# One low half of the transposed norm made on TensorE and copied by ScalarE, and the tile map of a routed mixture cut into four parts

## What is computed

```
x = x + ssm(layernorm(x))        # Bu = x B^T; h_t = a*h_{t-1} + Bu_t; y = h C^T + D*x
n = layernorm(x)
logits = n @ gate_w.T            # 8 experts
top_id, score = argmax(logits), sigmoid(max(logits))
x = x + swiglu_shared(n) + swiglu_{top_id}(n * score)   # hidden width 256
```

## Time and profile before

| | us |
|---|---|
| median of 3 runs | 280.53 (279.43 to 281.22) |
| the profiled execution | 280.06 |
| its span, first to last instruction | 277.8 |
| around the span | 2.26 |
| busy: PE / PEld | 235.3 (85%) / 181.2 (65%) |
| busy: DVE / ACT / POOL | 177.2 (64%) / 172.3 (62%) / 146.1 (53%) |

### The profile page before, as it was taken

How to read it: one execution, slowest core, us unless ns; L and a number is a source line. 1 busy time by engine, 2 the same in 40 slices (tenths; PEclk the granted TensorE clock), 3 DMA queues, 4 the chain that set the end, 5 groups by cost and what they waited for, 6 DMA issues and landing times. The chain is left out here.

```text
span 277.8 us, 6120 instructions
## 1 busy us (share of the span) xinstructions
PE 235.3 (85%) x1891; PEld 181.2 (65%) x1891; DVE 177.2 (64%) x512; ACT 172.3 (62%) x415; POOL 146.1 (53%) x150
## 2 busy tenths in 40 slices
PE   0595979979779999999599899999999999999900
PEld 0254466566457456767276799999999999765700
DVE  3799998799887976659952256655555565534200
ACT  2844898887897965633134889776777684523400
POOL 1000000027777757778781036777777777775950
PEclk9999597979999999999889999999999999999975
DMA  7999500002323222323944924454555443211992
GB/s 207 383 355 327 211 0 2 1 19 100 116 99 115 105 78 99 119 97 119 318 150 139 296 94 120 136 165 128 176 170 168 132 119 107 77 49 48 106 172 26
DMA packets 24862, 37.83 MB, mean 136 GB/s; under 512 B 3680, under 2 KB 16864, under 8 KB 24272
## 3 DMA queue, kind: packets, MB, share of 16 engines
q1 hardware_dynamic: 15264, 22.03, 25.9%
q0 software_dynamic: 9568, 15.41, 19.9%
HBM read 22.03 MB, written 19.73 MB: 150 GB/s over the span
## 5 line engine op out<-in xcount | busy, mean ns | idle before, releaser
L1045 POOL DMA_INDIRECT table<-rows,place x64 | 65.8, 1027 | 61.9 <-DVE place L815 43.0
L1086 POOL DMA_INDIRECT out<-w_full x51 | 49.3, 967 | 32.9 <-DVE w_full L1015 18.6
L441 PE MATMUL bank<-xT_hi,w_split 128*128 128x256 f16 (+1 forms) x156 | 41.1, 264 | 0.5 <-DVE xT_lo L1000 0.5
L443 PE MATMUL bank<-xT_hi,w_split 128*128 128x256 f16 (+1 forms) x156 | 41.1, 264 | 0.0
L442 PE MATMUL bank<-xT_lo,w_split 128*128 128x256 f16 (+1 forms) x156 | 40.9, 263 | 0.0
L593 ACT ACTIVATE n1T<-bank,g_scale 128x512 f32<-128x512 f32 x32 | 21.8, 687 | 28.8 <-PE bank L395 22.7
L453 PE MATMUL bank<-w_full,hid 128*128 x284 | 38.6, 277 | 0.2
L453 PEld LDWEIGHTS bank<-w_full,hid 128*128 128x128 f32 x284 | 34.8, 192 | 1.5 <-issue 0.4
L871 DVE SCALAR_TENSOR_TENSOR hid<-bank,h_scale,n1T 128x512 f32<-128x512 f32 x32 | 23.3, 747 | 15.3 <-ACT n1T L593 14.3
L407 PEld LDWEIGHTS bank<-w_full,hid 128*128 128x128 f32 x256 | 31.4, 195 | 2.1 <-issue 0.3
L407 PE MATMUL bank<-w_full,hid 128*128 128x128 f32 x256 | 31.5, 277 | 0.0
(11 more groups left out here) (142 smaller groups left out, 439.5 us busy)
## 6 DMA issues: line engine op xcount, KB each, us to landing
w_full<-table SPq DMA_DIRECT2D x24, 264.0 KB, 4.0
rows<-in_x SPq DMA_DIRECT2D x8, 512.0 KB, 7.6
w_full<-in_weights SPq DMA_DIRECT2D x3, 1152.0 KB, 12.0
table<-in_pads SPq DMA_DIRECT2D x1, 2112.0 KB, 9.2
table<-in_pads SPq DMA_DIRECT2D x8, 264.0 KB, 4.5
x_ring<-table SPq DMA_DIRECT2D x8, 264.0 KB, 3.8
out<-rows POOLq DMA_DIRECT2D x8, 256.0 KB, 7.9
table<-rows,place POOLq DMA_INDIRECT x64, 2.4
```

Source lines behind the costliest of these rows:

```text
L441: mm(o, w_of(kind, e, 0, c), xT_hi[k][:, 0:w], start=True, stop=False)
L443: last = mm(o, w_of(kind, e, 1, c), xT_hi[k][:, 0:w], start=False, stop=True)
L1045: g.indirect_dma_start(table[:, :], bass.IndirectOffsetOnAxis(ap=place[:, i:i + 1], axis=0), rows[:, i, :], None).then_inc(done, 16)
L1086: g.indirect_dma_start(out[:, :], bass.IndirectOffsetOnAxis(ap=x_in[k][:, s, 2 * D:2 * D + 1].bitcast(I32), axis=0), x_in[k][:, s, 0:D], N ...
```

## The change

1. `minus_one`, the identity times -1 in 16 bits, is made once by ACT in step -1, ahead of `norm1(0)`. `std1(1)` moves in ACT's step -1 from between `norm1(0)` and `copy_n1T(0,0)` to behind `copy_n1T(0,1)`.
2. Block 1 of every pair is no longer transposed by PE's transpose but by a matmul with the identity that opens an accumulation in bank 6. For pairs 0 to 6 PE then adds `minus_one` times `n2T_hi` to the bank (`rest_n2`), so the bank holds the low half, and ACT copies it to `n2T_lo` (`rest_lo`). DVE's `split_lo` makes the low half of block 0 alone, except in the last pair. `rest_n2(s-1)` stands on PE behind `skip(s+1)`; `rest_lo(s-1)` stands on ACT between `std2(s)` and `norm2(s,0)`. In step 7 `rest_n2(6)` comes behind `shared_gate_up(0)`.
3. `ranks(2)` moves on PE from ahead of `shared_down(1)` to behind `shared_down(0)`, and `places(2)` on DVE from behind the hidden values of block 2 to behind `base(0)`.
4. `tile_map` is cut in four, at b = 7, 9, 10 and 11, behind the hidden values of these blocks. The instructions are the same.

The core of the diff (the bodies of the map's parts are as they were):

```diff
             def transpose_n2(q, b):
                 pe.wait_ge(s_n2, q * 2 + b + 1)
-                after(pe, s_lo, q * 2 + b - 1)
+                after(pe, s_lo[b], q)
                 for t in range(BT):
                     i = q * PT + BT * b + t
-                    last = nc.tensor.transpose(bank[5 + b][:, P * t:P * (t + 1)], n2[:, i, :], identity)
+                    o = bank[5 + b][:, P * t:P * (t + 1)]
+                    if b == 0:
+                        last = nc.tensor.transpose(o, n2[:, i, :], identity)
+                    else:
+                        last = mm(o, n2[:, i, :], identity, start=(t == 0), stop=(t == BT - 1))
                 last.then_inc(s_t2, 1)
+            def rest_n2(q):
+                if q == 0:
+                    pe.wait_ge(s_minus, 1)
+                pe.wait_ge(s_hi, q * 2 + 2)
+                mm(bank[6][:], minus_one[:], n2T_hi[:, (q * 2 + 1) * SEQ:(q * 2 + 2) * SEQ],
+                   start=False, stop=True, skip_group_check=True).then_inc(s_rest, 1)
...
                     skip(s + 1)
+                if 1 <= s < LAST:
+                    rest_n2(s - 1)
...
             for b in range(FIRST):
                 shared_gate_up(b)
+                if b == 0:
+                    rest_n2(LAST - 1)
...
-                if b == 2:
-                    ranks(GROUPS - 2)
...
                     shared_down(b - 1)
+                if b == 1:
+                    ranks(GROUPS - 2)
...
+            def rest_lo(q):
+                act.wait_ge(s_rest, q + 1)
+                run(n2T_lo[:, (q * 2 + 1) * SEQ:(q * 2 + 2) * SEQ], bank[6][:], ACT.Copy).then_inc(s_lo[1], 1)
...
+                if s == -1:
+                    act.wait_ge(s_const, 16)
+                    run(minus_one[:], identity, ACT.Copy, scale=-1.0).then_inc(s_minus, 1)
                 if -1 <= s < LAST:
                     norm1(s + 1)
-                if s + 2 < PAIRS:
+                if s + 2 < PAIRS and s != -1:
                     std1(s + 2)
...
                     copy_n1T(s + 1, 1)
+                if s == -1:
+                    std1(1)
...
                     std2(s)
+                if s >= 1:
+                    rest_lo(s - 1)
                 if 0 <= s < LAST:
                     norm2(s, 0)
                     norm2(s, 1)
...
             def split_lo(q):
-                for b in range(2):
+                for b in range(2 if q == LAST else 1):
...
-                if b == 2:
-                    places(GROUPS - 2)
                 if 1 <= b <= EARLY:
                     base(b - 1)
+                if b == 1:
+                    places(GROUPS - 2)
...
                 if b == 7:
-                    tile_map()
+                    map_counts()
+                if b == 9:
+                    map_singles()
+                if b == 10:
+                    map_experts()
+                if b == 11:
+                    map_rows()
```

More of the change, by code:

```diff
@@ L114, in block_kernel @@
         d_diag = sb("d_diag", [P, P])
+        minus_one = sb("minus_one", [P, P], F16)
         w_max = sb("w_max", [P, 3])
@@ L223, in block_kernel @@
         s_r2, s_nb2, s_n2 = sem("r2_steps"), sem("nb2_ready"), sem("n2_ready")
-        s_t2, s_hi, s_lo = sem("n2_transposed"), sem("n2T_hi_ready"), sem("n2T_lo_ready")
+        s_t2, s_hi = sem("n2_transposed"), sem("n2T_hi_ready")
+        s_lo = [sem("n2T_lo_first_ready"), sem("n2T_lo_second_ready")]
+        s_minus, s_rest = sem("minus_one_ready"), sem("n2T_rest_ready")
         s_logit, s_route = sem("logits_ready"), sem("route_steps")
@@ L349, in logits @@
                     pe.wait_ge(s_parked, 2)
-                pe.wait_ge(s_lo, (g + 1) * GROUP * 2)
+                pe.wait_ge(s_lo[0], (g + 1) * GROUP)
+                pe.wait_ge(s_lo[1], (g + 1) * GROUP)
                 after(pe, s_before, g)
@@ L384, in shared_gate_up @@
                 tok = slice(block_of(b) * SEQ, (block_of(b) + 1) * SEQ)
-                pe.wait_ge(s_lo, block_of(b) + 1)
+                pe.wait_ge(s_lo[block_of(b) % 2], block_of(b) // 2 + 1)
                 for c in range(FC):
@@ L778, in split_lo @@
                     v.tensor_tensor(out=n2T_lo[:, tok], in0=bank[5 + b][:], in1=n2T_hi[:, tok],
-                                    op=ALU.subtract).then_inc(s_lo, 1)
+                                    op=ALU.subtract).then_inc(s_lo[b], 1)
             def route(g):
@@ L919, in _, with map_ready, map_spread, map_counts @@
                     route(s // GROUP - 1)
[L920 to L932, removed]
+            map_steps = [0]
+            def map_ready(instruction):
+                instruction.then_inc(s_map, 1)
+                map_steps[0] += 1
+                dve.wait_ge(s_map, map_steps[0])
+            def map_spread(values, n):
+                return values[:, None, :].to_broadcast([P, n, E])
+            def map_counts():
                 dve.wait_ge(s_count, 1)
-                ready(v.tensor_copy(pad_place[:], count_bank))
-                ready(v.tensor_tensor(out=count_f[:], in0=count_bank, in1=region_of, op=ALU.subtract))
+                map_ready(v.tensor_copy(pad_place[:], count_bank))
+                map_ready(v.tensor_tensor(out=count_f[:], in0=count_bank, in1=region_of, op=ALU.subtract))
                 v.memset(end_whole[:, 0:1], 0.0)
@@ L939, in tile_map @@
                 v.tensor_scalar(halves_i[:], count_f[:], float(P - 1), None, ALU.add)
-                ready(v.tensor_tensor(out=whole_i[:], in0=count_f[:], in1=round_up, op=ALU.add))
+                map_ready(v.tensor_tensor(out=whole_i[:], in0=count_f[:], in1=round_up, op=ALU.add))
                 v.tensor_scalar(halves_i[:], halves_i[:], P.bit_length() - 1, None, ALU.arith_shift_right)
-                ready(v.tensor_scalar(whole_i[:], whole_i[:], SLOTS.bit_length() - 1, None, ALU.arith_shift_right))
+                map_ready(v.tensor_scalar(whole_i[:], whole_i[:], SLOTS.bit_length() - 1, None, ALU.arith_shift_right))
@@ L943, in tile_map @@
                 v.tensor_copy(halves_f[:], halves_i[:])
[L944 to L949, removed]
@@ L950, in tile_map, with map_singles @@
-                ready(v.tensor_scalar(single[:], single[:], 0.0, None, ALU.max))
+                map_ready(v.tensor_copy(whole_f[:], whole_i[:]))
+                map_ready(v.tensor_tensor_scan(end_whole[:, 1:E + 1], ones_e, whole_f[:], 0.0, ALU.mult, ALU.add))
+            def map_singles():
+                map_ready(v.tensor_scalar(end_whole[:, 1:E + 1], end_whole[:, 1:E + 1], float(WHOLE), None, ALU.min))
+                map_ready(v.tensor_tensor(out=whole[:, 0:E], in0=end_whole[:, 1:E + 1], in1=end_whole[:, 0:E],
+                                          op=ALU.subtract))
+                map_ready(v.scalar_tensor_tensor(out=single[:], in0=whole[:, 0:E], scalar=-2.0, in1=halves_f[:],
+                                                 op0=ALU.mult, op1=ALU.add))
+                map_ready(v.tensor_scalar(single[:], single[:], 0.0, None, ALU.max))
@@ L951, in tile_map @@
                 v.tensor_scalar(first_single[:], whole[:, 0:1], 2.0, None, ALU.mult)
                 v.tensor_scalar(whole_gain[:], whole[:, 0:E], -2.0, float(PITCH), ALU.mult, ALU.add)
[L953 to L956, removed]
+                map_ready(v.tensor_tensor_scan(end_single[:], ones_e, single[:], 0.0, ALU.mult, ALU.add))
@@ new lines, in map_singles, with map_experts @@
+                map_ready(v.scalar_tensor_tensor(out=next_gain[:], in0=whole[:, 1:E + 1], scalar=2.0, in1=whole_gain[:],
+                                                 op0=ALU.mult, op1=ALU.add))
+                map_ready(v.tensor_tensor(out=single_gain[:], in0=next_gain[:], in1=single[:], op=ALU.subtract))
+            by_whole = (slice(0, WHOLE), end_whole[:, 1:E + 1], whole_gain[:])
+            by_single = (slice(WHOLE, TILES), end_single[:], single_gain[:])
+            def map_experts():
@@ L959, in tile_map @@
                     number = const[:, col["tile_no"]][:, 0:n]
-                    ready(v.tensor_tensor(out=ended[:, tiles, :], in0=spread(end, n),
-                                          in1=number[:, :, None].to_broadcast([P, n, E]), op=ALU.is_le))
-                ready(v.tensor_reduce(tile_expert_f[:], ended[:], AX, ALU.add))
+                    map_ready(v.tensor_tensor(out=ended[:, tiles, :], in0=map_spread(end, n),
+                                              in1=number[:, :, None].to_broadcast([P, n, E]), op=ALU.is_le))
@@ L963, in tile_map @@
+                map_ready(v.tensor_reduce(tile_expert_f[:], ended[:], AX, ALU.add))
                 for tiles, end, gain in (by_whole, by_single):
                     n = tiles.stop - tiles.start
-                    ready(v.tensor_tensor(out=ended[:, tiles, :], in0=ended[:, tiles, :], in1=spread(gain, n), op=ALU.mult))
+                    map_ready(v.tensor_tensor(out=ended[:, tiles, :], in0=ended[:, tiles, :], in1=map_spread(gain, n),
+                                              op=ALU.mult))
```

(13 more changed lines are left out.)

## The result

The changed kernel takes 290.31 us (median of 6 runs, 288.51 to 291.07), the kernel before 280.21 (6 runs, 279.19 to 281.38): 1.034 times as long, 95% interval 1.032 to 1.037. Where executions of a kernel fell into a longer group at a lower granted clock, ratios leave them out. The profiled execution took 290.9, its span is 288.7, so 10.9 more span than before.

A forecast was written before the change was run, and what follows sets the result against it. Pair stage bound by a loop through ACT, routed stage by PE and POOL, first tile by POOL's chain. 280.06 + 10.4 (POOL's chain) + 1.5 + 0.6 (clock) = 292.6, taken as 292.5 us; range 285 to 300.

The forecast's parts named there:

- The new wait: On ACT ahead of norm2(s), rest_lo waits for rest_n2 behind skip(s+1): second copy to norm2 4.5 us instead of 2.1.
- The length of the loop: ACT's pair-stage loop becomes 11.85 us; after five loops norm2(6) starts at 98.75 instead of 85.92, +12.8.
- What ACT waits for: Pair stage before: ACT idles once a step, 0.88 to 1.21 us for nb from DVE, with no other gap.
- std1's move: Kernel start: std1(1) behind the copy makes DVE's scan start 1.1 us later, carried on to norm2(0).
- POOL: Block 8's scatter at 113.7, POOL's chain +10.4 us, its two long scatters stay, tile at 164.8.
- a wait of several us: Sign on POOL: the scatter of block 8 would stand behind a wait of several us for place.
- The clock in the steps: Pair stage: more waiting of PE in every step lowers its clock; half of a full loss taken, 1.5 us.
- Rival C: Low clock in every pair-stage step: six losses of 1.5 us, 9 in place of 1.5, time 300; chance 0.14.
- The clock ahead of the tiles: PE waits about 3 us ahead of the first tile and its clock falls: 0.6 us lost.
- The map: Tile map in parts: stall of 3.44 and slow pitch go, 5.7 us off PE's chain, but this buys nothing.
- places: On DVE, place of group 2 comes 1.8 us sooner, ahead of two hidden values, for POOL's scatter of block 8.
- Rival A: Pair stage: DVE sets the pace, 0.6 us comes back each step, POOL's wait of 2.07 goes: 276.2; chance 0.06.

The follow-up runs named there:

- Run 1: Changed kernel with PE's rest product ahead of skip instead of behind it: 278.19 us, 0.996 of the kernel before.
- run 3: Changed kernel with std1(1) back in its old place, ahead of the first copy of n1T: 288.30 us, 1.034 of the kernel before.
- run 9: Kernel before with only the tile map cut in four parts, third chip: 279.88 us, 1.0034 of the kernel before.
- run 10: Kernel before with only places and ranks of the third group moved, third chip: 278.50 us, 0.9954 of the kernel before.
- runs 4: Kernel before with places and ranks moved and the tile map in four parts, no identity product: 279.39 us, 0.9995 of the kernel before.
- run 8: Changed kernel with rest product ahead of skip and std1(1) in its old place, on the slow chip: 332.08 us, 1.013 of the kernel before.
- run 12: Changed kernel with rest product ahead of skip and std1(1) in its old place, on the third chip: 278.02 us, 0.9959 of the kernel before.

## Why the prediction was right

290.3 was measured, 292.5 forecast, inside the range of 285 to 300, with the mechanism named. The profiled execution was 10.9 longer than before, where the sum had 12.5. Step by step:

- **The new wait** was as worked out, with its place. Forecast 4.5 us from the second copy to norm2; measured at full clock 99.82 + 0.50 - 95.88 = 4.4. Run 1 shows the cause: taking skip out of the wait alone brings the time back.
- **The length of the loop.** norm2(6) was forecast at 98.75 plus 1.5 of clock, 100.25; it came at 100.32. So close a match is in part luck: norm2(1) came 0.4 sooner than forecast (38.34), the three loops at full clock were 11.7, 12.0 and 11.6 long (forecast 11.85, though its own terms add up to 11.80), and the clock took 0.7 more than its term.
- **What ACT waits for.** "Everything else in ACT's step has no gap" holds for step 5, which was read, and not for all: in step 4 of the kernel before ACT also waited 0.74 us for PE's transposes (62.52).
- **std1's move**: forecast 1.1, measured 1.10 at norm2(0) in run 3.
- **POOL**: forecast 113.7 plus 1.5, 115.2, for the scatter of block 8; measured 115.65, behind `place`. The sign "a wait of several us" did not come: it was 2.78 us, before 2.37. POOL was free of its first 32 scatters at 112.86 and not at 107 to 109, since `keep_step` held it back for 2.32 and 2.14 us in them. Had `place` come much sooner still, no more than 2.5 us would have been gained. The 32 scatters from there took 42.8 us instead of 43.9, because their two long ones were shorter (4.0 together, before 5.4). This was the mis-sized term: I had kept both as they were. The tile followed the last scatter by 6.85 instead of 7.13 us, and so came at 165.30, not at 166.3.
- **The clock in the steps**: 1.5 forecast, 2.2 paid in this execution, by gaps 1.0 and 1.2 us longer. The granted clock, third number from the end, shows that the half level came in three stretches of the pair stage:

```profile
45.00:55.00 10.00, 8.88 (x93) 5.68 (x93) 5.16 (x23) 6.34 (x17) 0.00 (x0) 0.83 0.01 2
55.00:66.00 11.00, 8.30 (x41) 4.72 (x39) 8.96 (x32) 7.08 (x19) 0.00 (x0) 0.84 0.00 1
76.00:86.00 10.00, 8.78 (x90) 6.31 (x89) 6.05 (x28) 9.19 (x23) 6.08 (x7) 0.83 0.22 81
```

  Two of them fell on `bu` (2.80 and 2.84 us), which ACT waits for, the third (from 79.8) on `y` and the transposes, and cost ACT 0.15. In run 3's profiled execution there were three as well (from 39, 63 and 87), none on `bu`, and no gap grew. The half level is not new either: in the kernel before it lay on `bu` in steps 1 and 2, where ACT's gap was for DVE.

```profile
32.09 2.72 PE L318 MATMUL bank<-n1T,const 128*64 128x512 f32 x4
...
42.46 2.72 PE L318 MATMUL bank<-n1T,const 128*64 128x512 f32 x4
```

  So the change did not bring the low clock, it put `bu` at that clock on the path, and how often the two meet differs from one execution to the next. The term of 1.5 had its size by luck. Rival C wanted a loss in all six steps. The Trainium skill (TensorE: Matmul & The Clock Gate, HAM oscillation) tells of a kernel in which every burst of matmuls started at the lower level, each behind a wait for a DMA that was longer than the burst. Here, where PE waits 0.9 to 2.2 us a few times a step, it came three times in six steps.
- **The clock ahead of the tiles**: 0.6 forecast, nothing measured. PE idled 2.38 us there and the windows from 164 on stand at 1.00.
- **The map.** "Nine matmuls at a pitch of 0.43" was misread: the rows have six (137.25 to 139.81), so the slow pitch cost 1.3 us and not 1.9, and stall and slow stretch 5.1 and not 5.7; run 9 shows 5.3. "This gain buys nothing" was wrong as put: PE waited 2.38 us for the tile in the changed kernel, and with 5.3 us more in its chain it would have been 2.9 late. So within this change the parts of the map were worth some 3 us, worked out, not run. What run 9 shows is that they are worth nothing on the kernel before, where POOL's chain is as late as PE's.
- **places** gave 1.0 to 1.3 us alone, where the lateness of PE's chain, 0.81, was the expected cap. PE came to the tile's transposes 1.2 sooner in run 10: 0.7 is the wait for the tile that went, 0.5 that `shared_down(11)` was itself sooner in that execution (152.81, before 153.32), so the cap stands within the spread.

Rival A (DVE sets the pace) was right only in that DVE's `nb` had ended ACT's gap. With the product out of the way of skip, ACT still waits 0.81 us in most steps, now for PE, and the relief of DVE shows in no run's time.

## What to carry to other kernels

Where an engine works in program order, look at what stands ahead of the producer on its own queue, not at the cost of the producer: one 0.38 us matmul behind 2 us of unrelated matmuls, read by an engine with 1 us of slack, cost 10 us over six steps, and moving it by one line took all of it back. Taking a stall out of TensorE is worth only what the next wait leaves over, and the clock can take the rest: here the stall of 3.44 us came back as waits of 4.42 and 4.71 us with the half level behind them. After moving a consumer, list every reader of its output again.

## What the runs showed of the hardware

TensorE's clock behind a wait: with nothing issued for 4.42 and 4.71 us its next matmuls ran at the 1.2 GHz level for up to 6 us (runs 4 and 9), as after the 3.44 us stall before; with 2.38 us, and with matmuls of no use in the gap, at 2.4 GHz. Short waits don't rule the lower level out: in the pair stage of the changed kernel it came at 45.8, 59.4 and 79.8, and the two waits of PE next ahead of each were 0.9 us or shorter. What decides it there is not shown.

A scatter on POOL that begins while the large VectorE instruction on the routed weights runs (2.34 us, two operands from SBUF) ends about 0.85 us after that instruction. In the ten traces from outside the slow chip there are twenty, begun 0.27 to 1.27 us into it, and all ended 0.83 to 0.86 us after it. The twenty scatters begun 0.01 to 0.95 us ahead of it took their usual 0.97, even where they ran beside it nearly throughout, as the one at 138.69. VectorE's rows in the changed kernel, beside POOL's above: 138.70 + 2.34 = 141.04 against 139.97 + 1.92 = 141.89, and 149.81 against 150.67.

```profile
138.70 2.34 DVE L892 SCALAR_TENSOR_TENSOR w_split<-w_full,w_mul,w_split 128x2048 f16<-128x2048 f32 x1
...
147.47 2.34 DVE L892 SCALAR_TENSOR_TENSOR w_split<-w_full,w_mul,w_split 128x2048 f16<-128x2048 f32 x1
```

So the price of such a meeting, 1.0 to 1.9 us here, depends on the phase of the two. The Trainium skill (GPSIMD Engine Reference, Specifications) states that GpSimd's SBUF interfaces are shared with VectorE, with contention for VectorE instructions of two SBUF inputs; the delayed scatters agree, those begun just ahead of the instruction paid nothing.

And one chip of three ran the kernel before 17% slower (328.17 against 279.5 us), and the other four kernels tried on it 16 to 19% slower than elsewhere, with TensorE waiting for its own issue. The order of the kernels did not carry over: run 8's kernel was 1.3% slower than before there, and 0.4% faster on the third chip (run 12).
